# Other places for the small work of a two-layer graph network, and another order at its start

## The reference

```python
# layer 0, per node row; adj is 6144 x 6144, fp32
x_norm = layernorm(x, g_in, b_in)
gate   = hard gumbel choice from x_norm @ Wn + bn and u       # one number per node
view2  = (adj * gate[:, None] * gate[None, :]) @ x_norm
f      = sigmoid(concat(x_norm, view2) @ Wg + bg)
x      = layernorm(x + layernorm(f * (x_norm @ W1 + b1) + (1 - f) * (view2 @ W2 + b2) + x))
# layer 1: hyperbolic linear map of x to xt (tanh, artanh, Moebius sums), then
x      = layernorm(x + proj(expmap0(relu(logmap0(proj(expmap0(adj @ xt)))))))
```

## Time and profile before

| | |
|---|---|
| median of three runs | 966.04 us |
| the profiled execution: its time, its span | 968.86 us, 967.1 us |
| busy: PE, DVE, ACT, POOL | 912.5, 799.9, 691.1, 230.7 us |
| granted TensorE clock, mean over the span | 0.989 |
| moved over the span | 281.72 MB, 291 GB/s |
| chain that ended last, by engine | PE 47%, DVE 29%, ACT 8%, DMA 6%, POOL 5% |

### The profile page before, as it was taken

How to read it: one execution, slowest core, us unless ns; L and a number is a source line. 1 busy time by engine, 2 the same in 40 slices (tenths; PEclk the granted TensorE clock), 3 DMA queues, 4 the chain that set the end, 5 groups by cost and what they waited for, 6 DMA issues and landing times.

```text
span 967.1 us, 12611 instructions
## 1 busy us (share of the span) xinstructions
PE 912.5 (94%) x4052; PEld 724.1 (75%) x4052; DVE 799.9 (83%) x1791; ACT 691.1 (71%) x1224; POOL 230.7 (24%) x202
## 2 busy tenths in 40 slices
PE   5998998999999999999999999998999999899993
PEld 3555777777787877888888888886787778777882
DVE  4667888988898788978695775859999999989995
ACT  5775686868686657757565565655878989788993
POOL 2210211111111111111020010201100755484464
PEclk9999999999999999999999999999999999999997
DMA  6988697786868587868574574756899999899990
GB/s 242 376 289 309 237 401 274 293 309 256 324 242 339 226 306 255 312 219 303 208 277 164 218 288 175 255 196 223 315 376 370 383 388 413 342 376 381 397 361 33
DMA packets 51825, 281.72 MB, mean 291 GB/s; under 512 B 6528, under 2 KB 8496, under 8 KB 20656
## 3 DMA queue, kind: packets, MB, share of 16 engines
q1 hardware_dynamic: 46432, 271.48, 74.3%
q10 hardware_dynamic: 5328, 9.44, 2.6%
HBM read 271.44 MB, written 9.46 MB: 290 GB/s over the span
## 4 chain that ended last, share of the span: by engine, by line
PE 47%; DVE 29%; ACT 8%; DMA 6%; POOL 5%; issue 4%; SPq 0%; POOLq 0%; DVEq 0%; ACTq 0%
PE PS L1007 13%; PE PS L1009 13%; PE PS L1008 13%; DVE AL L742 8%; DVE XGL L742 7%; DMA A<-in_adjT_dram 4%; DVE XTL L742 2%; PE PS L1096 2%; PE PS L1092 2%; DVE BS L691 2%; PE PS L1005 2%; ACT AH L546 1%; POOL r_rs L436 1%; DMA FU<-in_x_dram 1%; POOL p_inv L436 1%
## 5 line engine op out<-in xcount | busy, mean ns | idle before, releaser
L546 ACT ACTIVATE AH<-A 128x1024 fp32r<-128x1024 f32 x251 | 257.3, 1058 | 112.0 <-PE PS L1009 84.6
L742 DVE TENSOR_TENSOR AL<-A,AH 128x1024 fp32r<-128x1024 f32 x251 | 299.4, 1220 | 41.9 <-ACT AH L546 40.8
L742 DVE TENSOR_TENSOR XGL<-A,XGH 128x1024 fp32r<-128x1024 f32 x119 | 139.2, 1217 | 5.0 <-ACT XGH L546 4.9
L1007 PE MATMUL PS<-AH,XGH 128*128 128x512 f32 x344 | 137.5, 400 | 6.2 <-DVE AL L742 6.2
L1009 PE MATMUL PS<-AH,XGL 128*128 128x512 f32 x344 | 134.5, 391 | 0.0
L1008 PE MATMUL PS<-AL,XGH 128*128 128x512 f32 x344 | 134.3, 390 | 0.0
L546 ACT ACTIVATE XGH<-A 128x1024 fp32r<-128x1024 f32 x119 | 118.5, 1056 | 7.9 <-DMA A<-in_adjT_dram 7.8
L1007 PE MATMUL PS<-AH,XTH 128*128 128x512 f32 x298 | 117.9, 396 | 5.5 <-DVE AL L742 5.4
L1009 PE MATMUL PS<-AH,XTL 128*128 128x512 f32 x298 | 116.7, 392 | 0.0
L1008 PE MATMUL PS<-AL,XTH 128*128 128x512 f32 x298 | 116.6, 391 | 0.0
L742 DVE TENSOR_TENSOR XTL<-A,XTH 128x1024 fp32r<-128x1024 f32 x92 | 109.7, 1220 | 4.9 <-ACT XTH L546 4.5
(11 more groups left out here) (242 smaller groups left out, 1545.5 us busy)
## 6 DMA issues: line engine op xcount, KB each, us to landing
A<-in_adjT_dram SPq DMA_DIRECT2D x243, 1024.0 KB, 6.8
GB<-gate_scratch SPq DMA_DIRECT2D x12, 256.0 KB, 3.8
XNT<-xnt_scratch SPq DMA_DIRECT2D x12, 256.0 KB, 4.2
XR<-in_x_dram SPq DMA_DIRECT2D x12, 256.0 KB, 4.9
x_scratch<-X SPq DMA_DIRECT2D x12, 256.0 KB, 7.6
xnt_scratch<-XNT ACTq DMA_DIRECT2D x6, 256.0 KB, 6.2
xnt_scratch<-X1T ACTq DMA_DIRECT2D x6, 256.0 KB, 5.5
XR<-in_x_dram ACTq DMA_DIRECT2D x4, 256.0 KB, 7.3
```

The source lines that it names most:

```text
L546: a.activation(high(m), A[:, n % RING, h * HW:(h + 1) * HW], ACT.Copy).then_inc(S["hi"], 1)
L742: v.tensor_tensor(low(m), A[:, n % RING, h * HW:(h + 1) * HW], high(m).bitcast(F32), ALU.subtract).then_inc(S["lo"], 1)
L1007: p.matmul(acc, hi[:, st], high(m)[:, mv], start=start, stop=False)
```

## The change

Four things, and the diff in full:

- The order at the start of row 0: VectorE takes chunk 2's statistics before it waits for the first logits, and ScalarE's first exp (which brings its table load) stands before the load of chunk 3 and the copy of chunk 0.
- In row 0's loop TensorE's first half of tile k stands ahead of the transposes of chunk k + 2, and the second half between these and the product with the logit columns.
- The tables of the first layer: most events move by one place, some by two or three (`part`, `resid`, `affine`, `curv1`, `curv2`, `scale`).
- The tables of the second layer hold two numbers, the second for the last two results. `tanh`, `norm`, `store` and `mean` come two places earlier. GpSimd's power has its own entry `rs`, and for the last two results `add` comes two places earlier and `take` one later.

```diff
--- before.py
+++ after.py
@@ -69,17 +69,18 @@
 LATE = 6
 RELOAD_AFTER = 4
 CLOSE = 12
-DVE_FIRST = {"m2m": (5, 0), "part": (4, 2), "gate": (3, 0), "q": (7, 0), "fuse": (9, 5), "stats1": (9, 7),
-             "nm1": (10, 9), "resid": (10, 9), "curv0": (14, 3), "affine": (11, 10), "stats2": (13, 10),
-             "curv1": (18, 13), "nm2": (14, 12), "curv2": (18, 13), "tc": (20, 15), "k": (20, 19), "beta": (22, 21),
+DVE_FIRST = {"m2m": (6, 1), "part": (7, 3), "gate": (4, 1), "q": (7, 1), "fuse": (10, 6), "stats1": (10, 8),
+             "nm1": (11, 9), "resid": (13, 9), "curv0": (14, 4), "affine": (13, 11), "stats2": (13, 11),
+             "curv1": (17, 15), "nm2": (14, 13), "curv2": (17, 15), "tc": (20, 16), "k": (20, 19), "beta": (22, 21),
              "xtl": (24, 22)}
-ACT_FIRST = {"mx": (2, 0), "tq": (9, 2), "tanh": (9, 5), "y1": (13, 10), "x1": (19, 14), "x1t": (19, 21),
-             "ln": (20, 16), "scale": (21, 21), "xth": (24, 23)}
-PE_FIRST = {"l0": (2, 0), "tr": (14, 12), "mx": (21, 19)}
-
-DVE_SECOND = {"take": 2, "floor": 8, "norms": 16, "coef": 16, "add": 19, "mean": 24}
-ACT_SECOND = {"relu": 7, "tanh": 15, "norm": 28, "store": 30}
-PE_SECOND = {"turn": 1}
+ACT_FIRST = {"mx": (3, 1), "tq": (9, 3), "tanh": (10, 6), "y1": (13, 11), "x1": (19, 15), "x1t": (19, 21),
+             "ln": (20, 17), "scale": (23, 21), "xth": (24, 23)}
+PE_FIRST = {"l0": (3, 1), "tr": (14, 13), "mx": (21, 19)}
+
+DVE_SECOND = {"take": (2, 3), "floor": (7, 8), "norms": (20, 15), "coef": (16, 15), "add": (19, 17), "mean": (22, 23),
+              "rs": (19, 18)}
+ACT_SECOND = {"relu": (7, 8), "tanh": (13, 13), "norm": (26, 26), "store": (28, 30)}
+PE_SECOND = {"turn": (1, 1)}
 
 
 def split_homes(halves, nch):
@@ -308,7 +309,7 @@
             out = {}
             for o, end in enumerate(ENDS):
                 for event, after in table.items():
-                    out.setdefault(end + after, []).append((event, o))
+                    out.setdefault(end + after[o >= NCH - 2], []).append((event, o))
             return out
 
         def last_place(*tables):
@@ -472,7 +473,7 @@
                     link(g.tensor_scalar(e["cf"], e["th"], MAX_NORM, None, ALU.min))
                     link(g.tensor_tensor(e["cf"], e["cf"], e["rc"], ALU.mult))
                     g.tensor_tensor(e["coef"], e["cf"], e["w"], ALU.mult).then_inc(S["coef"], 1)
-                if event == "add":
+                if event == "rs":
                     pow_half("v3", o + 1, e["rs"], e["v"], "rs3")
 
             events, results = first_places(DVE_FIRST), second_places(DVE_SECOND)
@@ -559,10 +560,10 @@
             gumbel_ln(0)
             normalize(0)
             gumbel_ln(1)
+            act.wait_ge(S["const"], 1)
+            a.activation(JUNK[:, 0:1], NHALF[:, 0:1], ACT.Exp)
             load_x(3)
             transposed(0)
-            act.wait_ge(S["const"], 1)
-            a.activation(JUNK[:, 0:1], NHALF[:, 0:1], ACT.Exp)
             store_xnt(0)
             normalize(1)
             gate_exp(0)
@@ -770,9 +771,9 @@
                                    in0=U[:, :].rearrange("p (b k) -> p b k", k=2), scalar=-1.0,
                                    in1=BNB[:, :].rearrange("p (o k) -> p o k", o=1).to_broadcast([P, NB, 2]),
                                    op0=ALU.mult, op1=ALU.add).then_inc(S["gumbel"], 1)
+            stats_pre(2)
             dve.wait_ge(S["gumbel"], 1)
             gate_begin(0)
-            stats_pre(2)
             gate_end(0)
             neg_mean_pre(2)
             stats_pre(3)
@@ -1053,14 +1054,14 @@
             transposes(1)
             rows_and_logits(1)
             for k in range(NCH):
+                if k + 1 < NCH:
+                    half(2 * k)
                 if k + 2 < NCH:
                     transposes(k + 2)
                 if k + 1 < NCH:
-                    half(2 * k)
+                    half(2 * k + 1)
                 if k + 2 < NCH:
                     rows_and_logits(k + 2)
-                if k + 1 < NCH:
-                    half(2 * k + 1)
             pe.wait_ge(S["gates"], NCH)
             pe.wait_ge(S["pre_xt"], NCH)
             p.transpose(PS[0:NB, 7, 0:P], GATE[:, :], ident).then_inc(S["gate_tr"], 1)
```

## The result

The change makes the kernel slower, by less than half a per cent: 972.02 us in the median against 968.30 of the kernel before, with the runs of both taken in the same comparison; ratio 1.0033, 95% interval 1.0019 to 1.0047. The profiled execution took 971.79 us (span 970.0). Three executions ran far slower than all others and are left out of the ratios: one of the kernel after (1031.83 us, granted clock 0.847), the profiled one of `e1_floor8` (1719.37 us, 0.82), for which reason that kernel has no row in the tables by stages, and one of the kernel before in the third set (3749.83 us).

A forecast was written before the change was run, and what follows sets the result against it. Bounds: TensorE in late rows, VectorE in stretches of early rows, TensorE, VectorE and transfers in the second layer. -1.4 - 5.2 + 1.2 + 2.5 + 1.0 = -1.9 us: 968.86 to 967.0, less 2.82 gives 964.1; 8-in-10 range 959.5 to 969.5.

The forecast's parts named there:

- the same within 0.5%: Whole kernel: time changes by no more than 0.5% (4.8 us); chance 0.68, against 0.23 faster and 0.09 slower.
- Row 0: Row 0's end: gates transposed 1.7 us earlier, TensorE's wait for the first `gate` product goes; -1.4 us, from -3.1 to 0.
- Rows 2 to 6: First layer's early rows: moved events remove VectorE idle, TensorE repays about 4.0 of 5.0 us waited; -5.2, from -6.5 to 0.
- Late rows and the seam: Rows 7 to 13: VectorE stands longer at `tc` and `nm1`, unhidden in row 12; +1.2 us, from -1.2 to +4.
- Second layer: Second layer: earlier `tanh` makes ScalarE wait for GpSimd's `floor`, delaying `relu`, roundings and TensorE; +2.5 us, from 0 to +7.
- The `tanh` term: Second layer's ScalarE: `tanh` two places earlier delays result 5 by up to 3.5 us, result 3 by 0.9; +2.5 in sum.
- The rival that came nearest: Result 5, around 855 us: ScalarE's stand at `tanh` stops TensorE over 2.3 us, clock falls; term 7.0, 968.6 us; chance 0.17.
- The clock: Seam, behind TensorE's 2.35 us wait at 675.20: half clock granted for a while, priced at 1.8 us over 652 to 740.
- The end: Last two results: `add` comes before `take`, so `take` is 2.1 us later; +1.0 us, from 0 to +2.1.

The follow-up runs named there:

- e1_floor8: The kernel after with the second layer's `floor` for results 0 to 9 put back from 7 to 8: 967.14 us, ratio 0.9963 to the kernel before.
- the third set: Runs changing the kernel before (968.06 us there): late rows' numbers, with `curv1`/`curv2` at 15 or 14; row 0 plus early rows; `tanh` at 13. Medians 967.71, 967.78, 961.03, 970.21 us.

## Why the prediction was wrong

**Where the 7.9 us between 964.1 and 972.02 lie.** 2.8 of them are the base: the forecast took 2.82 off the profiled execution to get to the median of three runs, 966.04, and 20 runs have their median at 968.30, close to that execution's 968.86. That part is bad luck; with the later median the forecast would be 966.4 and its range end at 971.8, so the result lies outside even then. 4.8 are the change itself, forecast as -1.9 and measured as +2.9 between the two profiled executions. The last 0.2 is the median of the kernel after above its own profiled execution. The call "the same within 0.5%", at 0.68 the likeliest, held.

**Row 0: right, little.** The loop kept its period: L735 comes at 57.66, 62.75 and 67.83 in the kernel after, 5.09 apart. The transpose of the gates came 1.3 us earlier (74.37 for 75.69; 1.7 was forecast), the first `gate` product at 87.46 for 88.51, not 86.8, with no wait of TensorE behind it. TensorE waits for row 1's first low part 3.59 us in place of 2.34, since VectorE's preparation of the weights didn't move, as was said. -1.4 was forecast; row 0 alone measured 0.9979 (-2.0, give or take 1.5), and in its profiled execution -0.9 up to half 48.

**Rows 2 to 6: right.** VectorE's idle before half 22 is gone: in row 3 of the kernel after, nothing on VectorE waits over 0.17 us from 196 to 222 us. Rows 2 and 3 were to be 1.5 to 2 us shorter; from `gate` to `gate` they are by 2.2 and 1.4. At TensorE's products, halves 48 to 168 take 231.0 us for 236.0, -5.1 where -5.2 was forecast; in all ten profiled kernels with the early numbers it is -4.8 to -5.3, in the other five within 0.2 of nothing. (The -7.9 of the first table is more because VectorE got further ahead and because row 1 is in it.) But the way to the figure was in part luck. The working let TensorE repay about 4.0 of the 5.0 us that it was seen to wait. After, that wait is

```profile
PE PS L1008 <- DVE AL L743: 3.6, 3, 1.3
```

so only 1.4 us of it went. Over the same 1032 matmuls TensorE's idle time of every kind fell from 7.1 to 5.5 us and its busy time from 229.0 to 225.5. Two things hide in that busy time. The one is the clock: behind a wait of 1.93 us at 165.9 TensorE was granted 0.86 of it from 160 to 170 in the kernel before. The kernel with `floor` 7 alone is the same there, has its clock at 1.00 after a wait of 1.95, and takes as long: what it doesn't lose by the clock it waits (idle 8.2, busy 227.8). The other is waits too short to be seen. A matmul is shown for 0.39 us and the next starts 0.23 later, so a wait of up to 0.16 between them vanishes in the overlap. Against the kernel with `floor` 7 alone, 2.7 of the 5 us went from shown idle time and 2.3 from within the busy time. The sum of shown waits was taken for a bound, and it is none.

**Late rows and the seam: right, low.** The idle at `tc` was forecast as about 1.5; it is 1.53 in row 12 and 0.90 in row 13, whose power is over four columns. `nm1` of row 12 waits 0.90 for its power at 661.88, as forecast. +1.2 forecast, +1.9 by the stages, and its cause shown by the kernel with `curv2` at 14 (-0.3).

```profile
677.50 0.17 DVE L882 TENSOR_TENSOR p_t<-p_n,p_inv 128x8 f32<-128x8 f32 x1 [1.53 <-POOL p_inv L437]
713.87 0.16 DVE L882 TENSOR_TENSOR p_t<-p_n,p_inv 128x4 f32<-128x4 f32 x1 [0.90 <-POOL p_inv L437]
```

**Second layer: this step failed.** It gave +2.5, at most +7, for `tanh`, and nothing for `floor`. Measured: by VectorE's low parts halves 360 to 485 lost 8.1 us, by TensorE's products 6.2; by the times `floor` costs 6.8 and `tanh` 3.3, 10 together. The `tanh` term was about right in sum (2.5 for a measured 1.0024 alone, 2.3 us) but placed wrongly: alone, it sits at result 3, where 0.9 was given, and not at result 5, where 3.5 was. In the kernel after, putting it back changes nothing at result 3 and much at result 5, where the inversion is too. ScalarE's wait at L657 for result 5, which was to be above 3 us, was 1.80. What was missing altogether is `floor`, from 8 to 7. The prediction went along ScalarE's queue and asked who stands behind `tanh`; it did not put the moved events of GpSimd beside each other, result by result, and so did not see that one place was the whole distance between `coef` and the next `floor`. "Others wait under 1 us, with roundings in store" was said of all other results, and result 1 is where TensorE lost 4 us.

**The rival that came nearest** was the slower one, 968.6, which is +2.6 us for a measured +2.9; that the sums agree is luck. It had a place (result 5, around 855), a stand over 2.3 us and the clock behind it, but gave ScalarE's `tanh` as its cause. At result 1 that falls: with `tanh` back at 15 the wait before `add` and the loss of TensorE's 4.3 us stayed. At result 5 it holds in part: there the loss shrank from 3.9 to 0.9. With the order restored and `tanh` still early it is gone as well (-0.8), and with `floor` 7 alone, `tanh` late, it is 5.2. So the inversion is enough for a loss there; how the two share it in the kernel after stays open.

**The clock.** It did fall where TensorE had stood. The kernel after, three windows behind the wait that ended at 781.52:

```profile
781.50:784.50 3.00, 2.98 (x7) 2.42 (x8) 3.00 (x4) 0.74 (x2) 2.71 (x4) 0.50 0.25 60
784.50:786.80 2.30, 2.30 (x7) 1.72 (x7) 2.30 (x3) 2.30 (x5) 0.41 (x1) 0.50 1.01 410
786.80:790.00 3.20, 3.20 (x15) 2.60 (x14) 3.20 (x6) 3.20 (x4) 0.00 (x0) 0.93 0.97 349
```

For 5.3 us TensorE had half its clock (1.2 GHz of 2.4), twelve matmuls 0.43 us apart instead of 0.23: 2.4 us on top of the 3.87 waited. VectorE's low parts, by which the stage is measured, came only 3.9 us later in all, TensorE's next products 4.3. So little of the 2.4 can have come on top of the wait there; this stall is never seen without the fall. Elsewhere the runs do have pairs. At the seam, which the prediction priced at 1.8 us, the kernel before waited 2.35 us at 675.2 and was granted 0.68 of its clock from 674.4 to 678.4; the kernel with row 0's change alone waited 2.33 at 674.4 and was granted 1.00 over the same four microseconds. Both took 80.4 us for halves 288 to 336. There the fall cost nothing in the end, because TensorE had to wait again later in that stage anyway: it was idle for 5.0 us of the stage in the one and for 6.2 in the other. Nor does the length of a wait settle whether the clock falls: it fell behind 1.93 us (the kernel before, 165.9), and stayed at 1.00 behind 2.33 us.

**The end: right, low.** +1.0, at most +2.1. From the last low part it is +1.5, from the end of the last product +1.9 (18.0 us for 16.1), from the cause that was named, since `take` in front of `add` gives it back. Two things add to the 1.0. The coefficient was to be there 0.5 us before the last product ended, as in the kernel before, and came with it (951.96 and 951.98). And `turn` of the last result took 1.11 us in place of 0.66, at a granted clock of 0.50, after TensorE had stood 3.40 us for `take`.

In sum, -1.9 became +2.9, counted on TensorE: row 0 and row 1 came 0.2 worse than forecast, rows 2 to 6 0.1 worse, rows 7 to 11 0.8 better (0 was given), the seam 0.7 worse, the second layer 3.7 worse, the end 0.9 worse.

## What to carry to other kernels

Where work is put on in-order engines by place numbers, write out the merged queue of each engine for every result, before and after, and look for pairs that change sides: a ready piece behind one that waits costs far more than its one place suggests, and two events in one place are kept in order only by a tie. Price a moved event by what it passes, not by how far it moves. Count what a stage won at the engine that bounds it; another engine that gets further ahead looks like a gain. And undo the parts one by one even when the whole is a loss: here the early rows alone are worth 0.9% by the times and 0.6% by the profiles, hidden under 1% lost by two numbers.

## What the runs showed of the hardware

The same small GpSimd instruction on 128x8 values took 3.16 us beside VectorE's low parts (at 767.01) and 0.24 in a pause of VectorE (at 855.94), both in the kernel after: a factor of 13. Over the profiled kernels it took 0.24 to 4.51 us. That the low parts cause this is read from what stands beside it; no run takes them away. The slower rival leaned on one such long instance at result 5 (3.30 us); in the kernel after that instance took 0.93, so a single long instance in one trace is poor ground for saying at which result a cost will fall.
